# Strassen-Winograd residual matmul on one core: x's first two tiles loaded as two transfers around W_e's first half, and the first quad's operand preparation re-ordered

## What is computed

```python
# x (128, 128, 512) f32, cond (128, 512), weight_matrix (1024, 512), W_proj (512, 512), b_proj (512,)
W_u, W_e = weight_matrix[:512], weight_matrix[512:]
u = gelu(cond @ W_proj + b_proj)                      # exact gelu
out = x + (u @ W_u)[:, None, :] + einsum('bnd,dc->bnc', x, W_e)
```

## Time and profile before

| what | us |
|---|---|
| median of 3 runs | 347.78 |
| the three runs | 347.91, 347.78, 345.88 |
| the profiled execution, device time | 345.7 |
| its span in the trace | 343.6 |
| TensorE matmul busy | 338.2 (98%) |
| GpSimd, VectorE, ScalarE busy | 283.8, 263.5, 248.9 |

### The profile page before, as it was taken

How to read it: one execution, slowest core, us unless ns; L and a number is a source line. 1 busy time by engine, 2 the same in 40 slices (tenths; PEclk the granted TensorE clock), 3 DMA queues, 4 the chain that set the end, 5 groups by cost and what they waited for, 6 DMA issues and landing times.

```text
span 343.6 us, 7875 instructions
## 1 busy us (share of the span) xinstructions
PE 338.2 (98%) x2703; PEld 329.1 (96%) x2703; DVE 263.5 (77%) x301; ACT 248.9 (72%) x428; POOL 283.8 (83%) x203
## 2 busy tenths in 40 slices
PE   8999999999999999999999999999999999999996
PEld 4768999999999999999999999999999999999996
DVE  2979987778977777887777788777788877778811
ACT  3667787787777778777777877777787777787741
POOL 2498999888898988889898888989888988888860
PEclk9999999999999999999999999999999999999999
DMA  7998799878789887878988787997878799787216
GB/s 259 309 198 197 171 245 232 219 199 209 197 169 243 227 216 191 221 183 183 244 215 217 191 218 182 198 244 207 219 185 213 181 216 242 200 210 207 92 48 230
DMA packets 73353, 70.64 MB, mean 206 GB/s; under 512 B 2944, under 2 KB 68480, under 8 KB 69248
## 3 DMA queue, kind: packets, MB, share of 16 engines
q1 hardware_dynamic: 73344, 70.53, 81.2%
HBM read 36.96 MB, written 33.55 MB: 205 GB/s over the span
## 4 chain that ended last, share of the span: by engine, by line
PE 90%; SPq 4%; DMA 2%; DVE 1%; ACT 1%; POOL 1%; issue 1%; ACTq 0%; DVEq 0%
PE banks L813 30%; PE banks L817 30%; PE banks L815 30%; DMA quad_raw<-in_x 2%; SPq L251 2%; SPq L270 1%; POOL lo L360 0%; POOL work L356 0%; SPq L267 0%; ACT hi L448 0%; DVE banks L570 0%; SPq L271 0%; DVE work L570 0%; SPq L260 0%; DVE banks L613 0%
## 5 line engine op out<-in xcount | busy, mean ns | idle before, releaser
L813 PE MATMUL banks<-t_hi,hi 128*128 128x256 f32 x496 | 140.5, 283 | 0.8 <-ACT banks L499 0.8
L815 PE MATMUL banks<-t_lo,hi 128*128 128x256 f32 x496 | 140.4, 283 | 0.0
L817 PE MATMUL banks<-t_hi,lo 128*128 128x256 f32 x496 | 140.4, 283 | 0.0
L815 PE MATMUL banks<-w_lo,hi 128*128 128x256 f32 x372 | 105.3, 283 | 0.0
L813 PE MATMUL banks<-w_hi,hi 128*128 128x256 f32 x372 | 105.3, 283 | 0.0
L817 PE MATMUL banks<-w_hi,lo 128*128 128x256 f32 x372 | 105.3, 283 | 0.0
L570 DVE STREAM_TRANSPOSE work<-quad_raw 128x1024 f32<-128x1024 f32 (+1 forms) x62 | 100.6, 1622 | 1.5 <-DMA quad_raw<-in_x 1.5
L813 PEld LDWEIGHTS banks<-t_hi,hi 128*128 128x128 f32 x496 | 95.2, 192 | 1.2 <-issue 1.2
L817 PEld LDWEIGHTS banks<-t_hi,lo 128*128 128x128 f32 x496 | 95.2, 192 | 0.0
L815 PEld LDWEIGHTS banks<-t_lo,hi 128*128 128x128 f32 x496 | 95.2, 192 | 0.0
L351 POOL TENSOR_TENSOR lo<-work,hi 128x1024 fp32r<-128x1024 f32 x31 | 74.9, 2416 | 17.5 <-ACT hi L438 17.5
(11 more groups left out here) (81 smaller groups left out, 411.0 us busy)
## 6 DMA issues: line engine op xcount, KB each, us to landing
out<-y SPq DMA_DIRECT2D x31, 1024.0 KB, 4.5
quad_raw<-in_x SPq DMA_DIRECT2D x120, 256.0 KB, 5.7
w_e<-in_L_cond_weight_matrix SPq DMA_DIRECT2D x2, 512.0 KB, 5.8
w_proj_sb<-in_L_cond_W_proj SPq DMA_DIRECT2D x2, 512.0 KB, 7.7
w_u<-in_L_cond_weight_matrix SPq DMA_DIRECT2D x1, 1024.0 KB, 8.7
quad_raw<-in_x SPq DMA_DIRECT2D x8, 128.0 KB, 8.2
out<-y SPq DMA_DIRECT2D x3, 256.0 KB, 2.1
head_raw<-in_x SPq DMA_DIRECT2D x1, 512.0 KB, 3.7
```

Source lines behind the costliest of these rows:

```text
L813: pe.matmul(psum[:, t, :], a_hi[:, 2 * j + t, :], b_hi[:, j, :], start=False, stop=False, skip_group_check=True)
L815: pe.matmul(psum[:, t, :], a_hi[:, 2 * j + t, :], b_lo[:, j, :], start=False, stop=False, skip_group_check=True)
L817: last = pe.matmul(psum[:, t, :], a_lo[:, 2 * j + t, :], b_hi[:, j, :], start=False, stop=(j == T - 1), skip_group_check=True)
```

## The change

Five edits go together. (1) Tile 0 is loaded alone ahead of W_e's first half and tile 1 between the halves, one transfer more on the queue. (2) TensorE flips tile 0 only ahead of the fillers; tile 0's first two products come next, then tile 1's flip, then the other products of blocks 0 and 1, then blocks 2 and 3; cond's flip comes later among them. ScalarE's casts and VectorE's splits in the head follow that order. (3) On VectorE the turn of tile 2 is ahead of cond's low part, tile 3's turn and split come later, and ScalarE's casts of tiles 2 and 3 move with them, tile 3's behind the copy of h. (4) t_sum[3] is formed on VectorE instead of GpSimd. (5) In the first quad, ScalarE's cast of s4 moves behind the L499 copy, and GpSimd's order becomes upper pair, t's fourth split, a22, s2, sum s4, s3, s4. All other quads keep their order.

```diff
+                sp.dma_start(direct[:, n, :], x[:, n, :]).then_inc(direct_loaded[n], 16)
                 load_w_e(n)
-            sp.dma_start(direct, x[:, 0:T, :]).then_inc(direct_loaded, 16)
...
-            pool.wait_ge(t_summed, 3)
-            pool.tensor_tensor(t_sum[:, 3, :, :], b21, t_sum[:, 1, :, :], ALU.subtract).then_inc(t_summed, 1)
...
                 if first:
                     split_t(3)
+                    split_a22()
                     split_s2()
                     sum_s4()
+                    split_s3()
+                    split_s4()
                 else:
                     sum_s4()
                     split_s2()
+                    split_s4()
+                    split_s3()
+                    split_a22()
...
+            direct_hi(0)
+            w_high(1)
+            direct_hi(1)
+            w_high(2)
+            w_high(3)
...
+            direct_hi(T)
             hi_t(0)
-            for n in range(T, HEAD):
-                direct_hi(n)
             act.wait_ge(h_summed, 1)
             act.copy(h[:, :], h_psum).then_inc(h_ready, 1)
+            direct_hi(T + 1)
...
                 act.copy(b_bank, a_bank[p]).then_inc(b_seeded, 1)
                 early = first and p == 0
+                if early:
+                    hi_s4(k, p, True)
...
             hi_s3(0, 0, True)
-            hi_s4(0, 0, True)
...
             split_direct(0)
+            split_w(0)
+            split_w(1)
             split_direct(1)
-            for j in range(NJ):
-                split_w(j)
+            split_w(2)
+            split_w(3)
...
+            dve.wait_ge(second_loaded, LOADS)
+            dve.wait_ge(direct_lo_ready, T)
+            turn_second(0)
             dve.wait_ge(cond_hi_ready, 1)
             dve.tensor_tensor(cond_lo, flip_psum, cond_hi.bitcast(F32), ALU.subtract).then_inc(cond_lo_ready, 1)
+            split_direct(T)
+            turn_second(1)
+
+            dve.wait_ge(t_summed, 3)
+            dve.tensor_tensor(t_sum[:, 3, :, :], w_e[:, 2:4, left], t_sum[:, 1, :, :],
+                              ALU.subtract).then_inc(t_summed, 1)
+            split_direct(T + 1)
             turn_up(0, 0, True)
...
+            pe.wait_ge(direct_loaded[0], 16)
+            flip(direct_psum[0], by_j(direct[:, 0, :]), direct_flipped)
             warm(WARM_ON)
...
+            pe.wait_ge(direct_hi_ready, 1)
+            pe.wait_ge(w_hi_ready[0], 1)
+            product(0, x_hi[0], w_hi, 0, first=True)
+            pe.wait_ge(w_hi_ready[1], 1)
+            product(0, x_hi[0], w_hi, 1)
+            pe.wait_ge(direct_loaded[1], 16)
+            flip(direct_psum[1], by_j(direct[:, 1, :]), direct_flipped)
+            pe.wait_ge(direct_lo_ready, 1)
+            for j in range(2):
+                product(0, x_lo[0], w_hi, j)
+            for j in range(2):
+                pe.wait_ge(w_lo_ready[j], 1)
+                product(0, x_hi[0], w_lo, j)
+            pe.wait_ge(direct_hi_ready, 2)
+            for j in range(2):
+                product(1, x_hi[0], w_hi, j, first=(j == 0))
+            for j in range(2):
+                product(1, x_hi[0], w_lo, j)
+            pe.wait_ge(direct_lo_ready, 2)
+            for j in range(2):
+                product(1, x_lo[0], w_hi, j)
+            for j in range(2, NJ):
                 pe.wait_ge(w_hi_ready[j], 1)
                 for t in range(T):
-                    if j == 0:
-                        pe.wait_ge(direct_hi_ready, t + 1)
-                    product(t, x_hi[0], w_hi, j, first=(j == 0))
+                    product(t, x_hi[0], w_hi, j)
+                for t in range(T):
+                    product(t, x_lo[0], w_hi, j)
+            pe.wait_ge(cond_loaded, 16)
+            flip(flip_psum, by_j(cond_sb[:, :]), cond_flipped)
+            for j in range(2, NJ):
+                pe.wait_ge(w_lo_ready[j], 1)
+                for t in range(T):
+                    last = product(t, x_hi[0], w_lo, j, last=(j == NJ - 1))
```

More of the change, by code:

```diff
@@ L152, in build_cond_residual @@
         w_e_loaded = [sem(f"w_e_loaded{n}") for n in range(2)]
-        direct_loaded = sem("direct_loaded")
+        direct_loaded = [sem(f"direct_loaded{t}") for t in range(T)]
         second_loaded = sem("second_loaded")
@@ L337, in _ @@
             b_of = w_e[:, :, :].rearrange("p (e j) (h c) -> p e h j c", e=2, h=2)
-            b11, b12, b21, b22 = b_of[:, 0, 0], b_of[:, 0, 1], b_of[:, 1, 0], b_of[:, 1, 1]
+            b11, b12, b22 = b_of[:, 0, 0], b_of[:, 0, 1], b_of[:, 1, 1]
             pool.wait_ge(proj_lo_ready, NJ)
@@ L361, in split_s2, with split_s4, split_s3, split_a22 @@
                                        ALU.subtract).then_inc(s2_lo, 1)
+                def split_s4():
+                    pool.wait_ge(s4_hi, k + 1)
+                    pool.tensor_tensor(slot(lo[p], S4), s4[p], slot(hi[p], S4).bitcast(F32),
+                                       ALU.subtract).then_inc(s4_lo, 1)
+                def split_s3():
+                    pool.wait_ge(s3_hi, k + 1)
+                    pool.tensor_tensor(slot(lo[p], S3), s3[p], slot(hi[p], S3).bitcast(F32),
+                                       ALU.subtract).then_inc(s3_lo, 1)
+                def split_a22():
+                    pool.wait_ge(a22_hi, k + 1)
+                    pool.tensor_tensor(slot(lo[p], A22), a22[p], slot(hi[p], A22).bitcast(F32),
+                                       ALU.subtract).then_inc(a22_lo, 1)
                 if first:
                     split_t(3)
+                    split_a22()
                     split_s2()
                     sum_s4()
+                    split_s3()
+                    split_s4()
                 else:
@@ L399, in direct_hi, with w_high @@
                 act.copy(x_hi[n // T][:, n % T, :, :], direct_psum[n % T]).then_inc(direct_hi_ready, 1)
-            for n in range(T):
-                direct_hi(n)
-            for j in range(1, NJ):
+            def w_high(j):
                 act.wait_ge(w_diag_ready, j)
                 act.copy(w_hi[:, j, :], w_e[:, j, :]).then_inc(w_hi_ready[j], 1)
+            direct_hi(0)
[3 more added lines that the diff above has]
+            w_high(3)
             for j in range(NJ):
@@ L742, in _ @@
             pe.wait_ge(ident_ready, 1)
-            for t in range(T):
-                pe.wait_ge(direct_loaded, 16)
-                flip(direct_psum[t], by_j(direct[:, t, :]), direct_flipped)
+            pe.wait_ge(direct_loaded[0], 16)
+            flip(direct_psum[0], by_j(direct[:, 0, :]), direct_flipped)
             warm(WARM_ON)
@@ L749, in product @@
                 return pe.matmul(banks[0][:, t, :], a[:, t, j, :], b[:, j, :], start=first, stop=last)
-            def high(j):
+            pe.wait_ge(direct_hi_ready, 1)
[6 more added lines that the diff above has]
+            pe.wait_ge(direct_lo_ready, 1)
```

## The result

The changed kernel takes 348.71 us (median of 15 runs, 347.48 to 350.56). The kernel before, run beside it, takes 345.76 (15 runs, 345.09 to 347.91): the 347.78 that the prediction started from was the median of three runs of which two lay in this upper tail. The ratio is 1.0079, 95% interval 1.0062 to 1.0096. The kernel got 0.8% slower: inside the 1% that one measurement tells, but with 15 runs the interval leaves no doubt of the sign. The forecast was 0.6 us faster, 347.2 with a range to 348.3; the measured time lies above it.

What follows compares the result with a forecast made beforehand. The prediction took the opening's last late start, hanging on the first quad's landing, as the bound. The first quad's new order gains 0.6 us, head and added transfer about nothing: 347.78 - 0.6 = 347.2, range 344.7 to 348.3.

Steps and rivals of the forecast that it cites:

- What bounds the kernel: Opening: the last late TensorE start, m6, hangs on VectorE's chain from the first quad's lower tiles landing near 21.49 us.
- Edit 5: First quad's order: the s4 cast behind L499 starts m6 at 29.77 instead of 30.55; gain 0.6 us, bounds 0.45 to 0.78.
- m6's gain would be cut by quad 1's L499: Quad 1: m6 can't start before 40.12, as VectorE's chain ahead of that copy is unmoved; gain cut from 0.78 to 0.58.
- The added transfer: SyncE's queue: one issue more, same bytes ahead; landing at 21.46 delayed 0 to 0.1 us, bounds -0.2 and 0.47.
- The prediction's own sign: First quad's landing at 21.46: moving by over 0.3 us, or a TensorE wait behind 42 us, would prove the forecast wrong.
- Rival (c): Transfer queue: loads cost by count; landing 0.95 later, 1.4 with the issue, 0.8 us slower, 348.6; chance 0.10.
- Paid in parallel: Transfer queue: the fixed cost of about 2.0 us per transfer overlaps, read from two transfers landing within 1.9 us.
- The head: Before m1: first product near 7.0, m1 near 26.2 instead of 26.75; nothing gained or lost at m6.
- Edit 4: VectorE before the first quad: t_sum[3] costs some 0.65 us, leaving 0.5 us of cover; GpSimd is freed 1.26.
- The starting point: Time of the kernel before: 347.78 us, the median shown, from which 0.6 was subtracted.
- cover: VectorE's spare time before the first quad's turn at 19.15: 0.5 us left after the added and moved work.

Runs made afterwards that it cites:

- run 16: Kernel before with tile 1 as its own transfer on ScalarE's queue, tile 0 and W_e's halves on SyncE's: 345.91 us, ratio 0.9992.
- run 7: Kernel before with W_u (1 MB) loaded as two transfers of 512 KB: 345.94 us, ratio 1.0000.
- run 15: Kernel before with W_e loaded as one transfer of 1 MB behind the pair of tiles: 345.32 us, ratio 0.9981.
- run 14: Kernel before with W_proj loaded as one transfer of 1 MB: 346.26 us, ratio 1.0014.
- run 8: Changed kernel with tiles 0 and 1 in one transfer again and t_sum[3] back on GpSimd: 345.45 us.
- run 2: Changed kernel with x's first two tiles in one transfer ahead of W_e again, all re-ordering kept: 345.92 us, ratio 1.0001.
- run 1: Kernel before with only the loads split (tile 0, W_e half 0, tile 1, W_e half 1): 348.16 us, ratio 1.0089.
- run 9: Kernel before with tiles 0 and 1 split, each behind its half of W_e: 349.23 us, ratio 1.0111.
- run 10: Changed kernel with each of tiles 0 and 1 loaded behind its half of W_e: 348.47 us, ratio to the kernel before 1.0090.
- run 4: Kernel before with the pair of tiles halved by partitions, W_e half 0 between, pieces still 4 KB: 348.88 us, ratio 1.0098.
- run 17: Kernel before with W_e in one transfer and the first quad's new order on ScalarE and GpSimd: 344.97 us, ratio 0.9979.
- b_split_ahead: Kernel before with tiles 0 and 1 in two transfers, both ahead of W_e's halves: 350.44 us, ratio 1.0136.

## Why the prediction was wrong

- **What bounds the kernel:** right. The gate was the landing, then VectorE. The table shows it one for one. (TensorE's waits hold a second entry, 1.2 us at the first filler, which no edit moved.)
- **Edit 5:** right in mechanism and, by the traces, in size: 0.58 in the changed kernel, 29.80 and 40.11 for 29.77 and 40.12 in its own run, 0.4 us in the medians (345.33 against 345.71), a little under the lower bound of 0.45. That m6's gain would be cut by quad 1's L499 was the step that made 0.78 into 0.58.
- **The added transfer:** the failed step. "The bytes ahead set the landing, and they are the same": they were, and the landing came 3.26 later. By the prediction's own sign (a landing moved by over 0.3) the forecast was wrong. I read a DMA share near 1 as a full rate, but GB/s beside it is the rate, and it fell to 212 at a share of 1.16. Rival (c) had the place and the sign. Its price was too small (0.95 for the transfer and 0.47 for the issue, of 3.26), and its reason, a cost by the count, doesn't hold either: the same count on another queue (run 16), or one more at W_u (run 7), costs nothing in the median, and cond in front costs 1.5 at the turn and 2.7 in the median at an unchanged count. That (c) gave 348.6 and 348.71 was measured is luck: its 0.8 of loss was added to a start 2.0 too high, where the measured loss is 2.95.
- **"Paid in parallel":** I put aside the Trainium skill's fixed cost per transfer ("DMA: Bandwidth & Descriptors", "Anatomy of one DMA") by one pair of landings. No run shows 2.0 us per transfer in series, so the rule as a serial price was rightly left; its advice in "Bandwidth", to batch transfers to 1 MiB, is borne out by run 15 (W_e, 345.32 against 345.89) and not by run 14 (W_proj, 346.26 against 345.89).
- **The head:** the first product came at 7.29 (predicted 7.0), but cond's low part was there only for 18.38 instead of 15.6, since VectorE's turn of tile 2 in front of it waited for the last transfer of `second` until 16.64. Edit 3 put a landing ahead of cond's low part; that cost 1.0 us on TensorE, hidden only because the gate was later still. "The head then gives nothing on top, and costs nothing" fails where the landing is in time: in run 8 the way from the first product (7.68) to the h stage (14.81) took 7.13 us instead of 6.17, with tile 1's flip inside, and m1 came 0.42 later than in the kernel before.
- **Edit 4:** the prediction gives no row for its 0.65. That is what such a subtraction takes with GpSimd idle (0.64), or with one operand in PSUM beside a GpSimd operation (0.67 at 17.66 in the changed kernel). On VectorE t_sum[3] reads two operands from SBUF while GpSimd works, and took 1.12 in the changed kernel and 1.77 in run 2. In run 2, with the landing in time, VectorE's queue held the lower turn by 0.93, more than the 0.58 of edit 5.
- **The starting point:** three runs were taken for the median. With 15, the kernel before is at 345.76. From there the same sum would have given 345.2, 3.5 under the measured 348.71; the 0.4 by which that lies above the stated range understates the miss.

What stays open is what the transfer engines do. The traces show rates and landings: in the runs with a 256 KB transfer among the first three on SyncE's queue the engines moved 212 to 294 GB/s from 12 to 16 us, against 329 in the kernel before. Run 16 is the exception: tile 0's 256 KB stood first there, and it was 330. So the size of one transfer isn't the whole condition. Why, and why it comes by chance in some executions of the other kernels, no run here tells.

## What to carry to other kernels

Where the chain that ends last begins at a landing, look at GB/s by stretch, not at the DMA share, and measure a change of the queue's first transfers by itself before building on it: here one transfer cut in two cost 2.5 us at the end by itself (run 1), two of W_e joined gained 0.6 (run 15), and two of W_proj joined gained nothing (run 14). A transfer needed earlier can go on another engine's queue. And before an operation is moved onto a queue with "cover", cost it by a row with operands in the same memories and with the neighbouring engine at work.

## What the runs showed of the hardware that was not expected

- Splitting the first 512 KB load of SyncE's queue in two made transfers issued 14 to 16 us later land 1.4 to 3.8 us later in the profiled executions (22.8 to 25.2 against 21.46), with pieces of 2 KB (runs 1, 5, 9, 10) and of 4 KB (run 4); on ScalarE's queue the same split cost 0.2 (21.70). W_e in one load of 1 MB landed whole at 6.8; in two, the halves landed at 6.6 and 7.9.
- The landing also moves by chance: 2 of 12 executions of b_w_u_split ran 1.5 us over its median, the profiled one with its turn 2.0 later; with W_e in one load all 11 lay within 0.32 (run 15), and again in run 17.
- VectorE's subtraction of two 128x512 f32 tiles in SBUF took 1.12 (changed kernel), 1.74 (run 10) and 1.77 us (run 2) beside GpSimd operations, where such a subtraction takes 0.64 with GpSimd idle (two splits of W_e in 1.28 at 7.67 in the changed kernel). The Trainium skill has the shared interface in "GPSIMD Engine Reference", section "Specifications": contention with VectorE instructions of two SBUF inputs. The rows agree.
- TensorE's wait from 4.7 to 6.8 in b_split_loads was followed by a granted clock of 0.65 from 8 to 12 us, a mean between its levels of 1.2 and 2.4 GHz: it was 0.50 from 8 to 10. In the changed kernel a wait of 0.85 ahead of 7.29 left it at 1.00, and so did a wait of 1.9 ahead of 9.52 in b_split_ahead.
